# Two heads in one 32-column strip of the value products, and one turn and one division per sequence

## The reference, cut to what matters

```python
# N_HEAD = 16, HEAD_DIM = 8, D_MODEL = 128
scores = jnp.einsum('bqhd,bkhd->bhqk', q, k) * scale
probs = jax.nn.softmax(scores, axis=-1)
attn = jnp.einsum('bhqk,bkhd->bqhd', probs, v).reshape(B, T, D_MODEL)
x = _layer_norm(src + attn @ Wo + bo, ln1_g, ln1_b)
# then each token goes through one of four experts (128 -> 512 -> 128), chosen by a router, and a second layer norm
```

## Time and profile before

| | us |
|---|---|
| median of three runs | 1488.88 |
| lowest and highest run | 1481.77 and 1491.17 |
| span of the profiled execution | 1560.5 |
| busy in that span: PE, PE's weight loads | 1172.4 and 759.1 |
| busy: DVE, ACT, POOL | 944.3, 819.0 and 691.4 |

### The profile page before, as it was taken

How to read it: one execution, slowest core, us unless ns; L and a number is a source line. 1 busy time by engine, 2 the same in 40 slices (tenths; PEclk the granted TensorE clock), 3 DMA queues, 4 the chain that set the end, 5 groups by cost and what they waited for, 6 DMA issues and landing times.

```text
span 1560.5 us, 30073 instructions
## 1 busy us (share of the span) xinstructions
PE 1172.4 (75%) x10624; PEld 759.1 (49%) x10624; DVE 944.3 (61%) x2991; ACT 819.0 (52%) x1850; POOL 691.4 (44%) x679
## 2 busy tenths in 40 slices
PE   4899999874466987988886676467779888987753
PEld 3666766562133645644554564332326545644553
DVE  5477777664467656667526885556667566663231
ACT  4666555452165756765662343224557657754532
POOL 5335345465122454454427676442133544543352
PEclk8799999975588978979987988756869879887977
DMA  8000000002222433343112110202234433432133
GB/s 250 2 2 1 2 2 2 2 1 81 84 83 76 134 108 118 117 137 126 45 53 71 41 50 22 71 21 72 74 102 134 125 108 117 125 106 84 37 99 104
DMA packets 116340, 116.72 MB, mean 75 GB/s; under 512 B 9288, under 2 KB 100040, under 8 KB 116040
## 3 DMA queue, kind: packets, MB, share of 16 engines
q1 hardware_dynamic: 101488, 74.84, 15.4%
q0 software_dynamic: 11008, 36.81, 7.2%
q10 hardware_dynamic: 3696, 3.15, 0.7%
HBM read 73.01 MB, written 42.15 MB: 74 GB/s over the span
## 4 chain that ended last, share of the span: by engine, by line
PE 53%; DVE 14%; issue 9%; DMA 7%; ACT 6%; SPq 4%; POOL 4%; another core or an unknown queue 3%; ACTq 0%; POOLq 0%; DVEq 0%
PE bank L1657 7%; PE bank L1695 7%; PE bank L1672 6%; PE bank L1716 6%; DVE NM L2276 3%; DMA scr_m<-MH 2%; SPq L741 2%; PE bank L1904 2%; PE bank L1480 2%; PE bank L1745 2%; PE bank L1734 2%; PE bank L1806 2%; PE bank L1722 1%; PE bank L1422 1%
## 5 line engine op out<-in xcount | busy, mean ns | idle before, releaser
L2276 DVE TENSOR_REDUCE NM<-bank 128x2 f32<-128x512 f32 x512 | 340.1, 685 | 233.0 <-PE bank L1722 195.4
L1244 ACT ACTIVATE PBS<-bank 128x512 f32<-128x512 f32 x512 | 300.0, 604 | 263.5 <-PE bank L1716 222.3
L1716 PE MATMUL bank<-QS,KS 50*128 50x256 bf16 x1024 | 201.4, 300 | 129.1 <-DVE NM L2276 64.3
L874 POOL TENSOR_TENSOR rs<-ve,half 128x4 f32<-128x4 f32 x88 | 90.0, 1023 | 434.3 <-DVE ve L2187 329.6
L1722 PE MATMUL bank<-KS,QS 48*128 48x256 bf16 x1024 | 210.7, 310 | 27.0 <-DVE NM L2276 17.1
L1716 PEld LDWEIGHTS bank<-QS,KS 50*128 50x128 bf16 x1024 | 66.4, 98 | 261.6 <-issue 153.2
L1695 PE MATMUL bank<-PBS,V 128*32 128x256 f32 x2048 | 163.9, 446 | 1.4 <-ACT PBS L1244 1.4
L983 POOL DMA_INDIRECT scr_x<-XS,POS x64 | 63.9, 998 | 82.5 <-DVE POS L2242 63.5
L1722 PEld LDWEIGHTS bank<-KS,QS 48*128 48x128 bf16 x1024 | 66.0, 99 | 55.8 <-DVE NM L2276 40.6
L1695 PEld LDWEIGHTS bank<-PBS,V 128*32 128x32 f32 x2048 | 59.2, 121 | 63.8 <-issue 35.1
L1218 ACT ACTIVATE HB<-bank,W 128x128 f32<-128x128 f32 x256 | 74.5, 396 | 24.1 <-PE bank L1657 19.9
(11 more groups left out here) (319 smaller groups left out, 2672.8 us busy)
## 6 DMA issues: line engine op xcount, KB each, us to landing
QS<-scr_q SPq DMA_DIRECT2D x64, 192.0 KB
KS<-scr_k SPq DMA_DIRECT2D x56, 192.0 KB
XD<-scr_x SPq DMA_DIRECT2D x16, 448.0 KB
scr_q<-PQ SPq DMA_DIRECT2D x32, 192.0 KB, 2.1
scr_k<-PQ SPq DMA_DIRECT2D x28, 192.0 KB, 2.1
scr_q<-PQ SPq DMA_DIRECT2D x32, 128.0 KB, 1.9
scr_y<-YB SPq DMA_DIRECT2D x16, 256.0 KB
scr_k<-PQ SPq DMA_DIRECT2D x28, 128.0 KB, 1.9
```

Source lines behind the costliest of these rows:

```text
L874: pool.tensor_tensor(rs_[:, :], ve_[:, :], half[:, 0:ve_.shape[1]], ALU.pow).then_inc(rstd_sem, 1)
L1244: act.activation(PB[i % PB_SLOTS][:, :, :], bank[1 + i % 2][:, :].rearrange("p (k t) -> p k t", k=2), ACT.Exp).then_inc(A.e, 1)
L1716: last_s = pe.matmul(bank[1 + s % 2][:, k * T:(k + 1) * T], KS[1 - par][r, b, s // 2, k * P:(k + 1) * P], QS[1 - par][r, b, s // 2, :], st ...
L2276: dve.tensor_reduce(NM[:, 2 * b + qt, h:h + 3:2], bank[3 + i % 2][:, :].rearrange("p (u t) -> p u t", u=2), AX_X, ALU.max, negate=True).th ...
```

## The change

The values' buffer gets 16 zero columns ahead of the first head. A product of the second group of four heads (`j` = 1) then takes as weights the 32 columns that begin 16 columns early: zeros of the head before, then its own eight values and the one. Both groups accumulate into the same 32 partitions: head `j` = 0 in columns 0 to 8 of the strip, head `j` = 1 in columns 16 to 24. So 16 heads (a sequence) fill bank 5, and the copies at slots 10 and 26 are gone. A turn takes four transposes for a whole sequence, not for one tile; a division takes the reciprocal of 32 sums and two products of 128 columns. There are two copies, two turns and two divisions for each pair. The number of value products and their shapes stay.

`sums0` is at slot 19 and `divide0` at 20 (21 in `TAIL`); `sums1` is at slot 3 (2 in `TAIL`) and `divide1` at 5. Bank 7 still takes the second sequence's turn; bank 0 is no longer used for a turn in `post`, and the wait for `E.pos`, which stood ahead of `turn3`, stands ahead of `anT`. `PA` of the one-head attention, which shared `OT1`, gets its own buffer, and ACT's wait ahead of its first use goes.

```diff
-AT = {..., "div2": 7, "div3": 8, ... "div0": 20, "div1": 27, ... "turn2": 4, "turn3": 8, ... "turn0": 19, "turn1": 24, ...}
+AT = {..., "divide1": 5, ... "divide0": 20, ... "sums1": 3, ... "sums0": 19, ...}
-TAIL = {..., "div2": 4, "div3": 6, ... "div0": 18, "div1": 25, ... "turn2": 2, "turn3": 7, ... "turn0": 20, "turn1": 23, ...}
+TAIL = {..., "divide1": 5, ... "divide0": 21, ... "sums1": 2, ... "sums0": 19, ...}
...
-        V1 = [sb(f"V1_{i}", [P, TP, H1, 32], scope=late) for i in range(2)]
+        V1 = [sb(f"V1_{i}", [P, 2 * D1 + TP * H1 * 32], scope=late) for i in range(2)]
+        VH = [v[:, 2 * D1:].rearrange("p (t h e) -> p t h e", t=TP, h=H1) for v in V1]
...
                     def copy_sums(i):
-                        h = {10: 0, 18: 1, 26: 2, 2: 3}[i]
-                        pair = c - 2 if i == 2 else c - 1
-                        if h % 2 == 0 and later(pair):
-                            act.wait_ge(A.pt, (pair - 1) * 4 + (h + 2))
-                        act.wait_ge(A.pv, c * 32 + (8 * h + 8 - (32, 64)[i == 2]))
-                        r = 2 * (h % 2)
-                        act.activation(OT1[h // 2][:, r:r + 2, :], bank[5][:, :].rearrange("p (r t) -> p r t", r=2),
+                        b = {18: 0, 2: 1}[i]
+                        pair = c - 1 - b
+                        if later(pair):
+                            act.wait_ge(A.pt, (pair - 1) * 2 + (b + 1))
+                        act.wait_ge(A.pv, c * 32 - (16, 32)[b])
+                        act.activation(OT1[b][:, :, :], bank[5][:, :].rearrange("p (q t) -> p q t", q=2),
...
                 def weigh(q, par, seq, b, s0):
                     pe.wait_ge(A.e, q + PV_GROUP)
-                    if s0 % 8 == 0:
-                        if later(seq * 2 + s0 // 8):
-                            pe.wait_ge(A.ocopied, seq * 2 + s0 // 8)
-                    at = s0 // 4 % 2 * T
+                    if s0 == 0:
+                        if later(seq):
+                            pe.wait_ge(A.ocopied, seq)
+                    at, j = s0 // 8 * T, s0 // 4 % 2
                     for kt in range(2):
                         for r in range(PV_GROUP):
-                            last = pe.matmul(bank[5][32 * r:32 * r + 32, at:at + T], V1[par][:, 2 * b + kt, s0 + r, :],
-                                             PB[(s0 + r) % PB_SLOTS][:, kt, :], start=(kt == 0), stop=(kt == 1))
+                            v = 2 * D1 * (1 - j) + ((2 * b + kt) * H1 + s0 + r) * 32
+                            last = pe.matmul(bank[5][32 * r:32 * r + 32, at:at + T], V1[par][:, v:v + 32],
+                                             PB[(s0 + r) % PB_SLOTS][:, kt, :], start=(kt == 0 and j == 0),
+                                             stop=(kt == 1 and j == 1))
...
-                def turn_sums(p, t, to):
-                    pe.wait_ge(A.ocopied, (p + g8) * 4 + (2 * (t // 2) + 2))
-                    for r in range(4):
-                        last = pe.transpose(to[:, r * P:(r + 1) * P],
-                                            OT1[t // 2][:, r, (t % 2) * P:(t % 2) * P + P], ident)
+                def turn_sums(p, b, to):
+                    pe.wait_ge(A.ocopied, (p + g8) * 2 + (b + 1))
+                    for t in range(2):
+                        for q in range(2):
+                            last = pe.transpose(to[:, (2 * t + q) * P:(2 * t + q + 1) * P],
+                                                OT1[b][:, q, t * P:(t + 1) * P], ident)
...
-                    def divide(p, t):
-                        ps = bank[7 if t == 2 else 0][:, :].rearrange("p (h e) -> p h e", e=32)
...
-                        link_n(dve.reciprocal(rec1[:, t, :], ps[:, :, D1]))
-                        dve.tensor_tensor(AN[:, t, :].rearrange("p (h e) -> p h e", e=D1), ps[:, :, 0:D1],
-                                          over(rec1[:, t, :].unsqueeze(2), [P, H1, D1]),
-                                          ALU.mult).then_inc(A.norm1, 1)
+                    def divide(p, b):
+                        ps = bank[7 if b else 0][:, :].rearrange("p (a r j e) -> p a r j e", a=4, r=4, j=2)
+                        sums = bank[7 if b else 0][:, :].rearrange("p (h e) -> p h e", e=2 * D1)[:, :, D1]
...
+                        link_n(dve.reciprocal(rec1[:, b, :], sums))
+                        rec = rec1[:, b, :].rearrange("p (a r j) -> p a r j", a=4, r=4)
+                        an = AN[:, 2 * b:2 * b + 2, :].rearrange("p t (q j r d) -> p (t q) j r d", q=2, j=2, d=D1)
+                        for j in range(2):
+                            last = dve.tensor_tensor(an[:, :, j, :, :], ps[:, :, :, j, 0:D1],
+                                                     over(rec[:, :, :, j].unsqueeze(3), [P, 4, 4, D1]), ALU.mult)
+                        last.then_inc(A.norm1, 1)
```

More of the change, by code:

```diff
@@ L392, in program @@
         PB = [PBS[:, 2 * T * i:2 * T * (i + 1)].rearrange("p (k t) -> p k t", k=2) for i in range(PB_SLOTS)]
-        OT1 = [sb(f"OT1_{i}", [P, 4, T], scope=late) for i in range(2)]
+        OT1 = [sb(f"OT1_{i}", [P, 2, T], scope=late) for i in range(2)]
+        PA = sb("PA", [P, TP, T], scope=late)
         QS.append(sb("QS1", [P, 2, H1 // 2, T], BF16, scope=late))
         KS.append(sb("KS1", [P, 2, H1 // 2, T], BF16, scope=late))
-        V1 = [sb(f"V1_{i}", [P, TP, H1, 32], scope=late) for i in range(2)]
+        V1 = [sb(f"V1_{i}", [P, 2 * D1 + TP * H1 * 32], scope=late) for i in range(2)]
+        VH = [v[:, 2 * D1:].rearrange("p (t h e) -> p t h e", t=TP, h=H1) for v in V1]
         Y1.append(sb("Y1_1", [P, TP, P], scope=late))
@@ L400, in program @@
         MH = [sb(f"MH{i}", [H1, 2, T], BF16, scope=late) for i in range(2)]
-        rec1 = sb("rec1", [P, TP, H1], scope=late)
+        rec1 = sb("rec1", [P, 2, 2 * H1], scope=late)
         AN = sb("AN", [P, TP, P], scope=late)
@@ L1323, in step @@
                             relu(n - 3, slot["relu"].index(i))
-                        if (i == 2 and post) or (i in (10, 18, 26) and att):
+                        if (i == 2 and post) or (i == 18 and att):
                             copy_sums(i)
@@ L1778, in step @@
                             last.then_inc(A.m1T, 1)
-                        if post and i == slot["turn2"]:
+                        if post and i == slot["sums1"]:
                             pe.wait_ge(A.vev, upto(0))
@@ L1782, in step @@
                                 pe.wait_ge(E.yused, upto(4) * 2)
-                            turn_sums(n - 2, 2, bank[7])
-                        if post and i == slot["turn3"]:
-                            pe.wait_ge(A.norm1, c * 4 - 6)
-                            if later(upto(3)):
-                                pe.wait_ge(E.pos, upto(3))
-                            turn_sums(n - 2, 3, bank[0])
+                            turn_sums(n - 2, 1, bank[7])
                         if pre and i == slot["x_turn"]:
@@ L1807, in step @@
                         if post and i == slot["anT"]:
-                            pe.wait_ge(A.norm1, c * 4 - 4)
+                            pe.wait_ge(A.norm1, c * 2 - 2)
+                            if later(upto(3)):
+                                pe.wait_ge(E.pos, upto(3))
                             turn(bank[0], AN, A.anT)
@@ L1850, in step @@
                             last.then_inc(A.m0T, 1)
-                        if att and i == slot["turn0"]:
+                        if att and i == slot["sums0"]:
                             pe.wait_ge(A.m0ev, upto(0))
@@ L1855, in step @@
                             turn_sums(n - 1, 0, bank[0])
-                        if att and i == slot["turn1"]:
-                            pe.wait_ge(A.norm1, c * 4 - 3)
-                            turn_sums(n - 1, 1, bank[0])
                         if post and i == slot["ranks"]:
@@ L2310, in step @@
                             split_max(c - 1, 1)
-                        if post and i in (slot["div2"], slot["div3"]):
-                            divide(n - 2, 2 if i == slot["div2"] else 3)
+                        if post and i == slot["divide1"]:
+                            divide(n - 2, 1)
                         if fin and i == slot["acc"]:
@@ L2344, in step @@
                                 choose(n - 2, par, link_key, k)
-                        if att and i == slot["div0"]:
+                        if att and i == slot["divide0"]:
                             divide(n - 1, 0)
-                        if att and i == slot["div1"]:
-                            divide(n - 1, 1)
                         if fin and i == slot["x_add"]:
```

28 lines of the change are left out of this document (13 added, 15 removed), and 18 rows, old and new, of tables (AT, START, TAIL).

## The result

The kernel after took 1476.39 us (median of 4 runs, 1472.45 to 1478.7) beside 1488.18 for the kernel before (4 runs, 1481.77 to 1491.17): a ratio of 0.9942 with a 95% interval of 0.9915 to 0.9969, 11.8 us less. The forecast was 1475. All 28 runs of the kernel after have a mean of 1479.9 us and the 64 runs of the kernel before beside them one of 1486.1, so the gain is nearer to 6 us than to 12 or to the forecast's 14.

The account below looks back on a forecast made before the run. PE was taken as the bound, with 53% of the chain. Terms 5.3 + 2.4 + 2.5 + 1.0 + 2.4 + 1.8 + 0.6 - 1.8 = 14.2 us less, from the median 1488.88 to 1475 us; range 1463 to 1490.

Parts of the forecast that it names:

- rival A: Only the second half of the steps counts, first halves end with POOL's scatters: gain 5.3 us, 1484 us; chance 0.18.
- turn 1: Four transposes at slot 24 (23 in the last steps) go: 0.44 us in 12 steps, 5.3 us gained.
- turn 3: Turn at slot 8 goes: 2.4 us in steps 2 and 3, 0 in 4 to 6, 2.5 in step 7.
- two waits that the profile gives to no engine: First half of steps 4 to 7: 4.53 and 2.09 us in step 5; PE work saved inside is worth nothing.
- Step 8: 2.4 + 1.8 us: Step 8, both layers: 2.4 us for two turns and two slot-10 copies, 1.8 of 7.3 for PE's wait to turn `AN`.
- rival B: Step 8's wait for the PE-to-DVE signal is saved whole, every term at its upper end: 22.5 us, 1466 us; chance 0.18.
- three-microsecond hop: Step 8: PE's signal to DVE for the reciprocal took three microseconds; worth 3.63 us a layer if all reaches the end.
- Step 9: 1.0 us, in one layer: Step 9, first layer: 0.64 us of turn and a reciprocal, less the longer division, 1.0 gained; second layer 0.
- Copies, 0.6: 32 of 64 ACT copies go, 19.4 us busy; beyond step 8 only 0.6 us on the chain, second layer's step 1.
- The second sequence's turn and division earlier, 1.8 us: Turn at slot 3 may wait for ACT's copy: 0.3 us in six steps, 1.8 lost; division at 5 in DVE's idle time.
- rival C: Turn at slot 3 waits 0.95 us in 12 steps, 11.4 against 5.3 gained: 6.1 us slower, 1495 us; chance 0.11.
- D, the clock: After the waits PE's clock stays low until as much work is done; 7.4 us of gain lost, 1482 us; chance 0.07.

Follow-up runs that it names:

- copies_back: Kernel after with two copies of 512 columns put back on ACT at slots 10 and 26, from a constant, read by nobody: 1485.72 us, 0.9972 of before.
- before_again: Kernel before, unchanged, run again for a second profile: 1484.78 us, 0.9985 of before; profiled span 1489.9 us.
- one_product: Kernel after with the division's two products of 128 columns made one of 256, output weight rows permuted to match: 1480.79 us, 0.9968 of before.
- late_turn: Kernel after with the second sequence's turn and division both at slot 8 (7 and 6 in the last steps): 1498.90 us, 1.0077 of before.
- slots_back: Kernel after with the second sequence's turn back at slot 4 and its division at 7: 1476.83 us, 0.9941 of before.
- divide_7: Kernel after with only the second sequence's division moved from slot 5 to 7, turn still at 3: 1482.07 us, 0.9983 of before.
- after_third: Kernel after, unchanged, run again beside three other kernels on the same chip: 1479.61 us, 0.9975 of before.

## Why the prediction came out, and what in it was wrong

The number held: 1476.39 in the comparison it was made for, against 1475, and both later medians of after lie in the range. That it came so near is in good part luck. Over all runs the gain is about 6 us and not 14.2, nearer to rival A's 5.3; and the sum did not hold term by term. Of the 10.2 us put into turn 1 and, in steps 2, 3 and 7, turn 3, 7.2 belong into the stretch from 2 to 7, which took 1.4 to 3.0 us longer. The stretches of steps 8 and 9 gave 8.9 to 11.2 us for the 7.0 put into them (4.2, 1.0 and 1.8 of turn 1).

*The bound.* "In steps 4 to 7 the chain holds two waits that the profile gives to no engine" was true of the earlier trace rows and of no other profile. From it came the 0 for turn 3 in steps 4 to 6. The prediction had named the other case ("if the wait were an artefact of profiling, 6 x 0.59 = 3.5"), and a span 71.6 us over the median was the sign that it should have been the main one. It made no difference in the end, for a reason that wasn't foreseen: nothing was gained there.

*Steps 2 to 7: 5.3 for turn 1, 2.4 and 2.5 for turn 3.* The turns are on the chain as read (eleven of 0.44, ten of 0.59), and this is the step that failed: an entry on the chain isn't yet a gain. Taken out, they leave 466.3 to 467.9 where there were 464.9 us; put back, 465.5 to 468.8. The prediction's own sign of this came, "the steps 3 to 7 shorter by less than 0.4 us each (the turn was no bound at all)"; step 7, where 2.5 us were to be gained, even takes longer (from 6 to 7). What is late next is probably the "exponential or the maximum of the slot two before", which the prediction named ("0 to 5.3") and priced at nothing. Rival A, near in size, kept the part that gave little, the second half.

*Step 8: 2.4 + 1.8 us.* Right in place and too small: 6.5 to 7.8 us, between the forecast's 4.2 and rival B's 9.7 (2.4 + 7.3). "`anT` has nothing left to wait for" is seen (739.62, no wait). The three-microsecond hop was an accident of that execution; the clean one has 0.67. "An end that goes with POOL, not with PE, keeps most of the gain for itself" was the wrong turn: the 15.9 us from the first scatter to the exponential of slot 10 were no fixed distance. In the clean trace of the same kernel they are 10.03 and 11.15, and `Z` there still waited for PE. It comes after 12.0 to 12.2 us in all three traces of after, and that is where POOL's row now sets the end.

*Step 9: 1.0 us, in one layer.* The two layers together gained 2.4 to 3.6. No row shows the cause. In its slots the trace speaks against the prediction, since `anT` waits longer than before (0.67), its one reciprocal standing behind DVE's routing work:

```profile
776.14 0.63 PE L1730 MATMUL bank<-W,OT 128*128 128x128 f32 x4 [0.87 <-ACT OT L1229]
778.19 0.66 PE L1736 MATMUL bank<-W,AN 128*128 128x128 f32 x4 [1.42 <-DVE AN L2260]
```

*Copies, 0.6 and part of step 8.* Beside PE in the middle steps, as said. In step 8 the copy at slot 10 cost nothing when it was put back at the full clock (12.21 us in the second layer of `copies_back`). In the first layer PE waits 0.68 and 0.40 us for the exponentials around it, but at a clock that had fallen before.

*Divisions.* 345 ns for 32 columns where 353 were expected from the earlier trace rows; DVE's busy time didn't fall, 948.5 against 947.8 us, though this group and its products are 7.9 us less than before; the rest of DVE varies by as much between traces (940.7 to 950.5 in kernels with the same divisions).
*The second sequence's turn and division earlier, 1.8 us.* At the turn PE waited 2.0 us in all, near the 1.8 put in for six of the steps, and far from rival C's 11.4, though three of the twelve waits are over the 0.3 of the test. "The division at 5 lies in DVE's idle time" didn't hold: it lies between two maxima, on the chain (the fence from 1213.41); that it costs some 4 us isn't shown.

*The rivals.* None came as written. D, the clock, has the right means and the wrong sign in step 8, where the level was higher in all traces of after; the last section has its other side.

What stays open: why the stretch from 2 to 7 gains nothing from 8.2 us of chain. DVE's waits (5.5 to 9.2 us more) fill the gap in size; that they fill it by cause is argued from the chain, not isolated. And what made step 8 long: each turn alone and both together left it short, and so did the copies in the layer with the full clock. How much of its 3.6 and 4.6 us is the low clock, which began ahead of all that was taken out there, and how much is the turn, the wait for its division and the copy, isn't separated; the second division was not put back, nor all of them together. Nor is it shown that the change is what keeps the clock up.

## What to carry to other kernels

Work taken off the engine that holds most of the chain can give nothing, as here in the middle steps: ahead of counting chain entries as gain, read whether a second engine's waits lie in the same slots. The gain can sit in one step out of eight, where the chain changes its engine, so compare before and after step by step and not by sums over the layer. A profiled execution some per cent over the median of the runs isn't the one to read unnamed waits from. A cause has to come first in time: a copy that ran 6 us after the clock fell didn't make it fall, though the two stood in the same step. And a producer has its best slot between two bounds: here turn and division at slot 8 cost 19 us, and a division at 5 came between maxima for which PE waits.

## What the runs showed of the hardware

The query projection that the change doesn't touch went from 765 ns a product to 853, 884 and 813 in the three traces of after. In steps 2 to 7 four, six and four of its groups took about 2 us and not 1.1. None did in `before_again`, in the three kernels with a turn put back or in the three with the division at 7; two did in `copies_back`, one in `one_product` and three in `late_turn`. The stretch ahead of such a group and its own, in after and then in `slots_back` (PE, PEld, DVE, ACT, POOL; then the granted clock):

```profile
1213.00:1217.30 4.30, 3.12 (x38) 1.38 (x36) 4.23 (x10) 4.11 (x9) 3.23 (x4) 1.00 0.30 95
1217.30:1220.30 3.00, 3.00 (x12) 1.52 (x14) 0.82 (x2) 1.59 (x4) 2.39 (x3) 0.51 0.23 65
```

```profile
1215.00:1219.40 4.40, 3.95 (x45) 1.82 (x44) 4.13 (x11) 4.40 (x12) 3.33 (x4) 1.00 0.29 99
1219.40:1221.00 1.60, 1.51 (x10) 0.84 (x13) 1.19 (x2) 0.93 (x3) 1.14 (x2) 1.00 0.14 46
```

In after PE was busy 3.12 of 4.30 us, fell to 0.51 (1.2 GHz) and did the projection there; in `slots_back` it was busy 3.95 of 4.40 and kept 1.00. So small changes of the work around go with another piece of work meeting the low level. Over the middle steps the low stretch mostly moves. In `before_again` the clock is at 0.50 earlier in the step, where the turn of slot 4 takes 1.04; in `divide_7` it is at 0.50 from 1208 to 1212. The mean clock of all runs says so too: 0.853 to 0.855 in the three sets of before that ran beside the experiments, 0.855 to 0.866 in the three sets of after, 0.851 in `divide_7`. Rival D's condition, a mean under 0.82, never came. The fall in after, behind the stretch in which PE did less, agrees with the section "What's actually happening" of "TensorE: Matmul & The Clock Gate" in the Trainium skill, that activity releases the throttle. Step 8 isn't explained by it: in the five us ahead of the first scatter and the two behind it PE is busy for the same time, within 0.02 us in each, in `before_again`'s first layer and in after's, and only the first then falls.

The clock is also a reason to compare many runs. Two executions of one kernel differ by up to 22 us (1471.65 to 1494.04 in `copies_back`), and the slow ones go with the low clocks: of the 31 runs of before beside `after_third` the fastest, 1474.71 us, had a mean of 0.873 and the slowest, 1494.72, one of 0.845.

And the level has its own weight: in step 8 `Z` comes 0.7 us later in `one_product`'s first layer, which falls to it for about 7 us, than in its second, which doesn't.
